# A select over a pad behind each gather, in place of the waits for landings

## The chip, the cores and the metric
The kernel runs on one core of one Trainium2 chip. The metric is the device time of one execution in microseconds. TensorE (PE) multiplies, VectorE (DVE) and ScalarE (ACT) evict and reduce, GpSimd (POOL) builds the indirect transfers, SyncE (SP) starts the plain ones.

## The reference
2048 samples, 40 categorical fields with 64 numbers each. For every pair of fields (780) and every sample a bilinear form is computed, then a small dense tower:

```python
e = jnp.stack([tbl_f[ids[:, f]] for f in range(40)], axis=1)     # (2048, 40, 64), written out in the reference
out = jnp.einsum('bie,fie,bif->bi', e[:, rowidx], param, e[:, colidx])   # 780 pairs, param (64, 780, 64)
h = jnp.concatenate([out, dense_ctx], axis=1)                    # (2048, 796)
h = jnp.maximum(h @ W_top1 + b_top1, 0.0)                        # 512
h = jnp.maximum(h @ W_top2 + b_top2, 0.0)                        # 256
y = h @ W_top3
```

Everything is float32.

## The kernel before
The batch is cut into four chunks of 512 samples (`NB`), each into four tiles of 128 (`BT`). Two fields make one tile `m` of 20. For chunk `c`, tile `m` the rows of two tables are fetched by 8 indirect DMAs (gathers), 4 for each of the two fields `f`, each of 128 rows of 64 numbers, into `rows[:, slot, t, ...]` (line 481). Tiles 4 to 7 of chunk 0 (`ONE_HOT`) are not gathered: their small tables are loaded whole, VectorE builds one-hot matrices (`one_hot`, line 647), and TensorE multiplies them with the tables (line 690). That leaves 76 gathered tiles, 608 gathers, in the order of `GATHERED`.

TensorE transposes a gathered tile (`transpose_tile`, line 701) when all its 128 counts have come (`pe.wait_ge(gathered[slot], use * 2 * BT * 16)`, line 698), and ScalarE copies it to `e_t` (line 502). A list `ITEMS`, written out ahead, fixes the order of the work on TensorE, VectorE and ScalarE; `TILE_AT` says before which item a tile is transposed. In chunk 0 the order of tiles is 4, 5, 6, 7, 0, 1, 2, 3 and then 8 to 19.

The items are "units" (line 727, two matmuls each, then VectorE multiplies into `prod`, lines 603 and 606, and TensorE sums with `strip` in `z_ps`, line 750) and "wides" for the pairs with tiles 0 to 3 (line 732, VectorE multiplies into `wide_prod`, line 619, ScalarE sums with an accumulator, line 541, in chunk 0 sometimes VectorE, line 630). No wide can start before tile 3 of its chunk is transposed. After each chunk the tower runs (lines 756, 760, 763, evicted at 550 and 553).

Weights come in pieces of up to 768 KB into three slots (`W_SLOTS`), started by SyncE when TensorE has used up the piece three before (line 421). Index lists are double-buffered by chunk (line 424).

GpSimd's whole program is the function below. At the start it makes `ident` and `first_row`. Then for each gathered tile it waits until the slot is free: tiles 0 to 3 have slots of their own for even and odd chunks, the others go round in six (`G_SLOTS`), each free when TensorE has transposed the tile that was in it (line 477). Then come four gathers of the first field and a wait until they have landed, four of the second and a wait until those have landed (line 487; only the very first four go without). Each gather adds 16 to the slot's semaphore when it has landed.

Of the kernel before, what the change touches and what calls it, by code (L numbers as in the profile page):

```python
# [7 lines left out]
ALU = mybir.AluOpType  # L8
# [3 lines left out]
P = 128  # L12
# [8 lines left out]
BT = NB // P  # L21
# [151 lines left out]
def through(n):  # L173

    return 2 * (n + 1)
# [78 lines left out]
def slot_of(tile):  # L254


    c, m = divmod(tile, TILES)
    if m < FIXED:
        return fixed_slot(c) + m, c // 2 + 1
    n = c * (TILES - FIXED) + m - FIXED - len(ONE_HOT)  # L260
    return 2 * FIXED + n % G_SLOTS, n // G_SLOTS + 1
# [78 lines left out]
def bilinear_tower(nc, tables, idx, hot_ids, dense_t, weights, w1z, b1c, w2p, b2c, w3c, out):  # L340
    with ExitStack() as ctx:
        def sb(name, shape, dt=F32):
            return ctx.enter_context(nc.sbuf_tensor(name, shape, dt))
# [4 lines left out]
        def sem(name):  # L348
            return ctx.enter_context(nc.semaphore(name))
# [15 lines left out]
        h2 = sb("h2", [P, KH2, NB])  # L365
        ident = sb("ident", [P, P])
        strip = sb("strip", [P, 62])
        first_row = sb("first_row", [P, 1], I32)
        first_row_f = sb("first_row_f", [P, 1])

# [15 lines left out]
        gathered = [sem(f"gathered{i}") for i in range(2 * FIXED + G_SLOTS)]  # L386
        w_in = [sem(f"w_in{i}") for i in range(W_SLOTS)]
        dense_in = sem("dense_in")
        hot_in = [sem(f"hot_in{i}") for i in range(len(ONE_HOT))]
        hot_ready = sem("hot_ready")  # L390
        hot_used = sem("hot_used")
        rows_known = sem("rows_known")
# [23 lines left out]
        @block.sync  # L416
        def _(sp):
            def load(piece):
                slot = piece % W_SLOTS
                start, n, _ = PIECES[piece]  # L420
                sp.dma_start(w[:, slot, :n * P], weights[:, start * P:(start + n) * P]).then_inc(w_in[slot], 16)

            def load_idx(c):
                sp.dma_start(idx_now[:, c % 2, :], idx[:, c * IDX:c * IDX + IDX]).then_inc(idx_in, 16)

            def load_tables(i):

                for h in range(2):
                    table = tables[2 * ONE_HOT[i] + h].rearrange("(p j) e -> p (j e)", j=HOT_J)
                    for part in (slice(0, HOT_SPLIT), slice(HOT_SPLIT, HOT_P)):  # L430
                        sp.dma_start(z_t[part, 2 * i + h, :], table[part, :]).then_inc(hot_in[i], 16)

            load_idx(0)
            for i in range(2):
                load_tables(i)
            load(0)
            for i in range(2, len(ONE_HOT)):
                load_tables(i)

            sp.wait_ge(transposed, T_NUMBER[0] + 1)  # L440
            load_idx(1)
            for piece in range(1, W_SLOTS):
                load(piece)
            for piece in range(W_SLOTS, len(PIECES)):

                sp.wait_ge(t_ready, through(PIECES[piece - W_SLOTS][2]))
                load(piece)
                if piece == MLP_BEHIND:
                    for dst, src in ((b1[:, :], b1c), (b2[:, :], b2c), (w3[:, :], w3c), (w2[:, :, :], w2p),
                                     (w1[:, :], w1z)):  # L450
                        sp.dma_start(dst, src).then_inc(mlp_in, 16)
                for c in range(2, CHUNKS):
                    if piece == IDX_BEHIND[c]:

                        sp.wait_ge(transposed, (c - 1) * TILES)
                        load_idx(c)

        @block.gpsimd
        def _(pool):
            nc.gpsimd.memset(ident[:, :], 0.0).then_inc(consts, 1)  # L460
            pool.wait_ge(consts, 1)
            nc.gpsimd.affine_select(out=ident[:, :], in_=ident[:, :], compare_op=ALU.not_equal, fill=1.0,
                                    base=0, pattern=[[-1, P]], channel_multiplier=1).then_inc(consts, 1)
            nc.gpsimd.iota(first_row[:, :], [[1, 1]], base=0, channel_multiplier=HOT_J).then_inc(rows_known, 1)
            pool.wait_ge(idx_in, 16)
            for tile in GATHERED:
                c, m = divmod(tile, TILES)
                slot, use = slot_of(tile)
                if c > 0 and m == 0:
                    pool.wait_ge(idx_in, 16 * (c + 1))  # L470
                if m < FIXED and use > 1:

                    pool.wait_ge(t_free, through(PLACE[c - 2, "wide", NW - 1]))
                elif use > 1:

                    last = max(t for t in GATHERED if t < tile and slot_of(t)[0] == slot)
                    pool.wait_ge(transposed, T_NUMBER[last] + 1)
                for f in range(2):
                    for t in range(BT):
                        col = (m * 2 + f) * BT + t  # L480
                        nc.gpsimd.indirect_dma_start(  # L481
                            out=rows[:, slot, t, E * f:E * f + E], out_offset=None, in_=tables[m * 2 + f],
                            in_offset=bass.IndirectOffsetOnAxis(ap=idx_now[:, c % 2, col:col + 1], axis=0),
                        ).then_inc(gathered[slot], 16)
                    if c > 0 or m > 0 or f > 0:

                        pool.wait_ge(gathered[slot], 16 * BT * (f + 1 + 2 * (use - 1)))

        @block.scalar
        def _(act):  # L490
# [69 lines left out]
            for n in range(ALL_ITEMS + max(GROUP_LAG) + 1):  # L560
                for tile in TILES_AT.get(n, ()):
                    prepare(tile)
                if n == NI:
                    act.wait_ge(mlp_in, 5 * 16)
                if n in STEPS_AT:
                    finish_step(*STEPS_AT[n])
                if n in TURNS_AT and n < ALL_ITEMS:
                    copy_half(TURNS_AT[n])
                for c, t in Z_ORDER:
                    if t < ZS and group_at(c * GROUPS + Z_FIRST[t + 1] - 1) == n:  # L570
                        copy_z(c, t)
                done = n - REDUCE_LAG
                if 0 <= done < ALL_ITEMS and ITEMS[done][1] == "wide":
                    c, _, v = ITEMS[done]
                    if not reduced_by_vector(c, v):
                        reduce(c, v)
# [334 lines left out]
```

## Time and profile before

| what | value |
|---|---|
| median of 3 runs | 1275.0 us (1274.24 to 1276.26) |
| profiled execution | 1274.63 us, span 1272.8 us |
| TensorE busy | 1231.0 us, 97% |
| VectorE, ScalarE busy | 1023.4 and 1023.9 us, 80% each |
| GpSimd busy | 577.7 us, 45%, of which 608 gathers 576.9 us |
| mean granted TensorE clock | 0.993 |

The span is the time from the first to the last instruction of the profiled execution. GpSimd's busy time counts the making of the transfers' descriptors, not the transfers. "Idle before" in a group of instructions is the time the engine stood still ahead of them, with the releaser that ended it; "issue" is a gap for which the profile shows no wait. The chain of waits follows what released what back from the last instruction. Only what stands on it sets the time.

### The profile page before, as it was taken

To read this page: it belongs to the slowest core of one execution; us is meant where nothing else is said; L and a number is where in the kernel's file an instruction comes from. 1 tells how busy PE (TensorE), PEld (TensorE's weight loads), DVE (VectorE), ACT (ScalarE), POOL (GpSimd) and SP (SyncE) were. 2 spreads that over 40 slices of the span, in tenths; PEclk is the share of its full clock that TensorE was granted. 3 is DMA by queue.
4 is the path that set the end of the run, shared out by engine and by line. 5 is a ranking of instruction groups with operands and counts; after the bars stand their busy time and mean duration, and the time that the engine had idled before them with its cause. 6 is when DMAs were issued, how large, how long until landed. Compare 5 with 4: busy or idle time off the path is not lost.

```text
span 1272.8 us, 23705 instructions
## 1 busy us (share of the span) xinstructions
PE 1231.0 (97%) x6064; PEld 481.1 (38%) x6064; DVE 1023.4 (80%) x1680; ACT 1023.9 (80%) x7945; POOL 577.7 (45%) x615
## 2 busy tenths in 40 slices
PE   6788999999999999999999999999999999999999
PEld 3233433333333343333344333433343333343333
DVE  5768999998887777888787887788889787788980
ACT  0049988777488989998958999899968898999981
POOL 5555555555555555555345555555225554000000
PEclk9989999999999999999999999999999999999999
DMA  6311422132221222222221222122112122111100
GB/s 173 94 46 46 143 72 70 45 94 64 71 70 48 70 71 70 49 67 64 66 67 47 73 69 71 45 70 72 54 59 69 46 70 67 30 47 50 44 2 0
DMA packets 33201, 80.88 MB, mean 64 GB/s; under 512 B 11773, under 2 KB 12285, under 8 KB 32937
## 3 DMA queue, kind: packets, MB, share of 16 engines
q1 hardware_dynamic: 12320, 57.17, 13.9%
q0 software_dynamic: 19456, 19.96, 7.7%
q10 hardware_dynamic: 1288, 2.24, 0.6%
q8 instruction: 48, 0.79, 0.3%
q14 instruction: 89, 0.72, 0.2%
HBM read 79.32 MB, written 0.01 MB: 62 GB/s over the span
## 4 chain that ended last, share of the span: by engine, by line
PE 60%; ACT 31%; issue 3%; DMA 2%; POOL 2%; DVE 1%; another core or an unknown queue 1%; ACTq 0%
ACT wide_prod L541 29%; PE ring L727 26%; PE z_ps L750 13%; PE ring L732 11%; PE ring L756 7%; DMA rows<-tbl,idx_now 2%; POOL rows L481 2%; PE ring L701 2%; ACT e_t L502 1%; PE ring L760 1%; DMA idx_now<-idx 0%; DVE prod L606 0%; PE ring L763 0%; PE ring L708 0%
## 5 line engine op out<-in xcount | busy, mean ns | idle before, releaser
L541 ACT ACTIVATE wide_prod<-wide_prod 128x64 f32<-128x64 f32 x3904 | 933.7, 243 | 52.4 <-DVE wide_prod L619 25.6
L481 POOL DMA_INDIRECT rows<-tbl,idx_now x608 | 576.9, 949 | 496.7 <-DMA rows<-tbl,idx_now 292.2
L541 ACT ACTIVATION_READ_ACCUMULATOR wide_prod<-wide_prod 128x1 f32 x3904 | 739.4, 189 | 24.4 <-issue 23.4
L606 DVE TENSOR_TENSOR prod<-ring,e_t 128x512 f32<-128x512 f32 x1008 | 630.8, 683 | 147.6 <-PE ring L727 101.1
L727 PE MATMUL ring<-e_t,w 64*128 64x512 f32 x2176 | 563.0, 609 | 9.6 <-ACT e_t L502 5.9
L619 DVE TENSOR_TENSOR wide_prod<-ring,rows 128x512 f32<-128x512 f32 x512 | 328.3, 682 | 44.6 <-PE ring L732 33.3
L727 PEld LDWEIGHTS ring<-e_t,w 64*128 64x128 f32 x2176 | 215.9, 187 | 300.1 <-issue 203.7
L732 PE MATMUL ring<-w,e_t 64*128 64x512 f32 x1024 | 292.1, 607 | 11.4 <-ACT e_t L502 7.1
L750 PE MATMUL z_ps<-prod,strip 128*32 128x512 f32 x2096 | 256.2, 603 | 0.1
L732 PEld LDWEIGHTS ring<-w,e_t 64*128 64x128 f32 x1024 | 106.2, 186 | 147.0 <-issue 86.7
L750 PEld LDWEIGHTS z_ps<-prod,strip 128*32 128x32 f32 x2096 | 55.3, 109 | 182.0 <-issue 119.6
L502 ACT ACTIVATE e_t<-ring 128x512 f32<-128x512 f32 x80 | 44.7, 587 | 90.7 <-PE ring L701 47.9
L756 PE MATMUL ring<-z_t,w 128*128 128x512 f32 x224 | 99.8, 598 | 0.0
L756 PEld LDWEIGHTS ring<-z_t,w 128*128 128x128 f32 x224 | 41.4, 190 | 56.8 <-issue 49.2
L603 DVE TENSOR_TENSOR prod<-ring,e_t 64x512 f32<-64x512 f32 x80 | 54.8, 685 | 6.2 <-PE ring L727 3.9
L701 PE MATMUL ring<-ident,rows 128*128 128x128 f32 x304 | 45.5, 284 | 7.8 <-DMA rows<-tbl,idx_now 7.8
L701 PEld LDWEIGHTS ring<-ident,rows 128*128 128x128 f32 x304 | 32.5, 142 | 49.8 <-issue 41.2
L514 ACT ACTIVATE z_t<-z_ps 128x512 f32<-128x512 f32 x20 | 11.8, 588 | 38.8 <-PE z_ps L750 30.1
L690 PE MATMUL ring<-wide_prod,z_t 125*64 125x512 f32 x128 | 30.5, 631 | 10.7 <-DMA z_t<-tbl 10.7
L550 ACT ACTIVATE h<-ring,b 128x512 f32<-128x512 f32 x16 | 10.9, 683 | 27.9 <-PE ring L756 27.8
L647 DVE TENSOR_SCALAR wide_prod<-h,first_row_f 125x512 f32<-125x512 int32 x48 | 20.4, 490 | 12.1 <-DMA z_t<-tbl 8.3
L760 PE MATMUL ring<-h,w 128*128 128x512 f32 x64 | 29.2, 602 | 0.0
(23 smaller groups left out, 79.3 us busy)
## 6 DMA issues: line engine op xcount, KB each, us to landing
w<-weights SPq DMA_DIRECT2D x64, 768.0 KB
rows<-tbl,idx_now POOLq DMA_INDIRECT x608
w<-weights SPq DMA_DIRECT2D x4, 512.0 KB
z_t<-tbl SPq DMA_DIRECT2D x8, 224.0 KB
w<-w1z SPq DMA_DIRECT2D x1, 1792.0 KB
h<-hot_ids ACTq DMA_DIRECT2D x6, 256.0 KB
z_t<-hot_ids ACTq DMA_DIRECT2D x2, 256.0 KB
w<-w2p SPq DMA_DIRECT2D x1, 512.0 KB
```

The source lines that it names most:

```text
L481: nc.gpsimd.indirect_dma_start(out=rows[:, slot, t, E * f:E * f + E], out_offset=None, in_=tables[m * 2 + f], in_offset=bass.IndirectOffse ...
L502: nc.scalar.activation(e_t[:, m, :], ring[:, BANKS["tile", tile][0], :], ACT.Copy).then_inc(e_ready, 1)
L541: last = nc.scalar.activation(products, products, ACT.Copy, accum_out=z_b[:, h, t, col:col + 1])
L603: nc.vector.tensor_tensor(dst[half, 0, :], ring[half, bank, :], e_t[half, m - 1 + j, :], ALU.mult).then_inc(t_free, 1)
L606: nc.vector.tensor_tensor(dst[:, j, :], ring[:, bank, :], e_t[:, k, :], ALU.mult).then_inc(t_free, 1)
L619: nc.vector.tensor_tensor(dst[:, j, :, :], src[:, bank, :, :], rows[:, fixed_slot(c):fixed_slot(c) + FIXED, t, :], ALU.mult).then_inc(t_fr ...
L701: last = nc.tensor.transpose(dst[:, P * t:P * t + P], rows[:, slot, t, :], ident[:, :])
L727: nc.tensor.matmul(dst, w[field, slot, P * o:P * o + P], e_t[field, m - 1 if diagonal and b == 0 else m, :], start=True, stop=True).then_i ...
L732: nc.tensor.matmul(dst, e_t[field, m, P * t:P * t + P], w[field, slot, P * o:P * o + FIXED * P], start=True, stop=True).then_inc(t_ready, 1)
L750: last = nc.tensor.matmul(z_ps[32 * col:32 * col + 32, :], strip[:, 30 - 2 * r:62 - 2 * r], prod[:, (c * NU + UNIT_PLACE[c][u]) % PROD_SLO ...
L756: return nc.tensor.matmul(dst, w1[:, t * H1 + P * h:t * H1 + P * h + P], z_t[:, Z_NUMBER[c, t] % Z_SLOTS, :], start=start, stop=stop)
L760: return nc.tensor.matmul(dst, w2[:, k, P * h:P * h + P], h1[:, k, :], start=k == 0, stop=k == KH1 - 1)
```

## The change
The two landing waits per tile go. In their place GpSimd runs one select over a 128x256 float32 tensor `pad` behind each gather, that is 608 of them. Nobody reads `pad`. Each select waits for the one before it (semaphore `paced`), since it writes what it reads. The other waits of GpSimd (index lists, free slots) are as before, and so is TensorE's wait for a whole tile.

```diff
+        pad = sb("pad", [P, 2 * P])
...
+        paced = sem("paced")
...
+            nc.gpsimd.memset(pad[:, :], 0.0).then_inc(paced, 1)
+            paused = 1
             pool.wait_ge(idx_in, 16)
...
                         ).then_inc(gathered[slot], 16)
-                    if c > 0 or m > 0 or f > 0:
-
-                        pool.wait_ge(gathered[slot], 16 * BT * (f + 1 + 2 * (use - 1)))
+
+                        pool.wait_ge(paced, paused)
+                        nc.gpsimd.affine_select(out=pad[:, :], in_=pad[:, :], compare_op=ALU.not_equal, fill=1.0, base=0,
+                                                pattern=[[-1, 2 * P]], channel_multiplier=1).then_inc(paced, 1)
+                        paused += 1
```

## Rows read from the trace of the kernel before

**Rows 1.** The page: busy us, share of the span, instructions of each engine.
```profile
PE 1231.0 (97%) x6064; PEld 481.1 (38%) x6064; DVE 1023.4 (80%) x1680; ACT 1023.9 (80%) x7945; POOL 577.7 (45%) x615
```

**Rows 2.** The page: the chain that ended last, by engine.
```profile
PE 60%; ACT 31%; issue 3%; DMA 2%; POOL 2%; DVE 1%; another core or an unknown queue 1%; ACTq 0%
```

**Rows 3.** The chain in order of time: start us, us, what.
```profile
63.18 2.44 DMA rows<-tbl,idx_now
```

**Rows 4.** GpSimd's waits (us in total, times, longest) and line 481's durations.
```profile
POOL rows L481 <- DMA rows<-tbl,idx_now: 292.2, 142, 5.9
POOL rows L481 <- issue: 139.3, 457, 0.3
POOL rows L481 <- PE ring L701: 55.6, 5, 28.8
...
L481 POOL DMA_INDIRECT rows<-tbl,idx_now x608: 938/944/1316, 4.9 to 1074.2; - x152
```

**Rows 5.** Timeline of TensorE, 44 to 80 us: start us, us, instruction, idle before.
```profile
55.88 1.99 PE L727 MATMUL ring<-e_t,w 64*128 64x512 f32 x8 [0.69 <-ACT e_t L502]
65.67 1.12 PE L701 MATMUL ring<-ident,rows 128*128 128x128 f32 x4 [7.80 <-DMA rows<-tbl,idx_now]
67.47 2.08 PE L727 MATMUL ring<-e_t,w 64*128 64x512 f32 x4 [0.69 <-ACT e_t L502]
69.47 3.64 PE L750 MATMUL z_ps<-prod,strip 128*32 128x512 f32 x16
...
75.87 1.92 PE L750 MATMUL z_ps<-prod,strip 128*32 128x512 f32 x16
```

**Rows 6.** Timeline of GpSimd: gathers 1, 32, 33 and 208.
```profile
4.92 1.11 POOL L481 DMA_INDIRECT rows<-tbl,idx_now  x1 [3.37 <-DMA idx_now<-idx]
...
63.18 0.94 POOL L481 DMA_INDIRECT rows<-tbl,idx_now  x1 [0.30 <-issue]
65.88 0.94 POOL L481 DMA_INDIRECT rows<-tbl,idx_now  x1 [1.75 <-DMA rows<-tbl,idx_now]
...
356.81 0.94 POOL L481 DMA_INDIRECT rows<-tbl,idx_now  x1 [0.30 <-issue]
```

**Rows 7.** Timeline of GpSimd, its first instructions.
```profile
0.25 0.10 POOL L898 MEMSET const-float32-0.0<- 128x1 f32 x1 [0.25 <-issue]
...
0.74 0.20 POOL L460 MEMSET ident<- 128x128 f32 x1 [0.29 <-POOLq L898]
1.19 0.28 POOL L462 TENSOR_SCALAR_AFFINE_SELECT ident<-ident 128x128 f32<-128x128 f32 x1 [0.24 <-POOL ident L460]
1.44 0.12 POOL L464 IOTA first_row<- 128x1 int32 x1
```

**Rows 8.** Line 647, the one-hots: ns least/median/most, first and last start.
```profile
L647 DVE TENSOR_SCALAR wide_prod<-h,first_row_f x48: 468/481/689, 10.1 to 33.8; 125x512 f32<-125x512 int32 x48
L647 DVE TENSOR_SCALAR wide_prod<-z_t,first_row_f x16: 478/480/689, 36.9 to 43.4; 125x512 f32<-125x512 int32 x16
```

**Rows 9.** Groups by line, GpSimd, 4 to 43.8 us.
```profile
L481 POOL DMA_INDIRECT rows<-tbl,idx_now x21 | 23.2, 1103 | 19.1 <-DMA rows<-tbl,idx_now 10.9 <-issue 4.9 <-DMA idx_now<-idx 3.4
```

**Rows 10.** Stretches: us, busy PE, PEld, DVE, ACT, POOL (x), granted clock, DMA share, GB/s.
```profile
58.00:63.00 5.00, 0.00 (x0) 0.00 (x0) 1.52 (x3) 0.00 (x0) 2.83 (x3) 0.99 0.55 173
63.00:73.30 10.30, 6.95 (x26) 2.07 (x28) 0.12 (x1) 0.60 (x1) 5.60 (x6) 0.51 0.11 21
```

**Rows 11.** Timeline of TensorE: transposes of chunk 1, tiles 8 and 9, then 11.
```profile
363.25 1.09 PE L701 MATMUL ring<-ident,rows 128*128 128x128 f32 x8
...
392.83 0.66 PE L701 MATMUL ring<-ident,rows 128*128 128x128 f32 x4
```

**Rows 12.** Groups by line, VectorE: 200 to 300 us, then 1080 to 1170 us; engines in 200:300.
```profile
L606 DVE TENSOR_TENSOR prod<-ring,e_t 128x512 f32<-128x512 f32 x112 | 69.5, 682 | 3.5 <-PE ring L727 3.4
...
L606 DVE TENSOR_TENSOR prod<-ring,e_t 128x512 f32<-128x512 f32 x75 | 47.2, 683 | 13.4 <-PE ring L727 13.4
...
200.00:300.00 100.00, 100.00 (x554) 38.51 (x551) 94.62 (x156) 79.62 (x628) 55.87 (x60) 1.00 0.24 67
```

## The prediction

> **What bounds the kernel now.** I read the page first. TensorE is busy 97% of the span, VectorE and ScalarE 80% each, GpSimd 45% [rows 1]. The chain that ended last gives TensorE and ScalarE 91% of the span and the gathers, DMA and GpSimd together, only 4% [rows 2]. Its pieces in order of time say where that 4% lies: the last landing on it begins at 63.18 with tile 3's last gather and ends at 65.62; after that there are only matmuls, evictions and reductions [rows 3]. So the gathers decide when the dense part starts, and nothing later, as long as none of them comes late.
>
> GpSimd's waits look large, 292.2 us for landings in 142 waits, 139.3 us of "issue" in 457 gaps, 55.6 us for slots that TensorE has not emptied [rows 4]. Almost none of it is on the path: TensorE waits for a landing once, 7.80 us, before it transposes tile 3 at 65.67 [rows 5]. What the change can win is inside that one wait and the slow clock around it. What it can lose is the lead of the gathers over TensorE further on.
>
> **What GpSimd does per gather now.** In a quiet stretch the timeline shows 0.94 us for a gather, 0.30 us until the next, and after four of them a landing wait of about 1.7 us [rows 6]. That is 3 x 1.24 + 0.94 + 1.75 = 6.41 us for four, 1.60 each. Some waits are longer, up to 5.9 us [rows 4], so that from 65.88 (33rd gather) to 356.81 (208th) the mean is 290.93/175 = 1.66, and from 4.92 to 63.18 (32 gathers) it is 58.26/31 = 1.88 [rows 6].
>
> **Removed.** 151 landing waits, the 142 that cost something together 292.2 us of GpSimd's time [rows 4]. Nothing on another engine read them; TensorE has its own wait on the same counts.
>
> **Added.** 608 selects of 128x256, each behind a wait for the select before it. That wait is for an instruction that ended a whole gather earlier, so I cost it at nothing; were its cover gone it would be the 0.24 us that stand between the ident memset and its select [rows 7]. The select itself is not in the trace at this size. At 128x128 it takes 0.28 us, the 128x1 memsets 0.10 to 0.12, so 128 columns cost about 0.17, and 256 columns 0.28 + 0.17 = 0.45 [rows 7]. The iota behind it starts 0.03 before the select's end, so what it occupies is about 0.42. Bounds: below, 0.28 + (0.20 - 0.10), the memset's slope, less 0.03 = 0.35; above, twice the 128x128 one, 0.56. I take 0.42.
>
> The gaps are the disputed term. The 0.30 us between two gathers may lie behind a gather (then it stays once), before a gather (then it can hide under the select), or on both sides of any pair (then it comes twice). After a landing, and likewise after the memset, an instruction starts 0.24 to 0.26 us after what it waited for, whatever it is; the iota starts behind the select with no gap. I take the gap once. Pace: 0.94 + 0.30 + 0.42 = 1.66, bounds 0.94 + 0.35 = 1.29 and 0.94 + 0.60 + 0.56 = 2.10. A useful way to see the change: the pace of before is 1.60 and stalls on top, the new one 1.66 and none.
>
> The Trainium skill ("GPSIMD Engine Reference", Performance pitfalls for Q7 kernels) has a compare-and-select loop at 1.03 to 2.03 cycles an element at 1.2 GHz: 0.22 to 0.43 us for 256 columns. By its lower figure the pace would be an estimated 1.46, by its upper 1.67; the row's slope, 0.17 for 128 columns, is 1.3 ns a column and stands nearer the upper one.
>
> **The start.** VectorE builds the one-hot tables from 10.09 to 44.12 with 64 instructions of about 0.48 us, up to 0.69; gathers beside them go from 0.944 up to 1.316 [rows 8, 4]. Over the first 21 gathers their mean is 1.103, so that is 21 x 0.159 = 3.3 us in all [rows 9]. It stays. The selects may be held up too: some 17 fall beside these instructions; at none it costs 0, at a whole 0.48 each it costs 8. I take 0.13 each, 2.2, for 5.5 together (bounds 3.3 and 11.5). Tile 3 lands with its 32nd gather, 2.44 us after its start [rows 3]:
>
> 4.92 + 31 x 1.66 + 5.5 + 2.44 = 64.3 us, 1.3 us before today's 65.62.
>
> Tiles 0 to 2 are no limit: TensorE's one landing wait was for tile 3, and tile 2 would be there eight gathers, 13 us, before it, at about 51, while TensorE is still at work up to 57.87 [rows 5].
>
> Then the clock. TensorE does nothing from 58 to 63 us, the granted clock falls, and from 63.0 to 73.3 it is 0.51, the 1.2 GHz level [rows 10]. The work in it is slow: four L727 matmuls 2.08 us against half of 1.99, sixteen L750 3.64 against 1.92, the transpose 1.12 against 0.66, together 3.3 us on the chain [rows 5]. Tile 3 comes 1.3 us earlier and the work before it somewhat later (VectorE's one-hots are held up by the selects as well), so the idle stretch is shorter. No row shows whether the clock then holds; bounds are 0 and 3.3 and I take 2.5. Gain at the start: 1.3 + 2.5 = 3.8 us. Behind it ScalarE's reductions and TensorE's matmuls make up the chain, 91% of it, so it is carried to the end [rows 2].
>
> **The lead further on.** The tightest place is chunk 1, tile 9, the 26th gathered: last gather at 356.81, transposed as the second of the two that begin at 363.25, so at about 363.7 [rows 6, 11]. Its landing would be 4.92 + 207 x 1.66 + 5.5 + 2.44 = 356.5; TensorE wants it at 363.7 - 3.8 = 359.9. It holds by 3.4 us. Tile 11 (223 intervals) lands at 383.0, wanted at 389.0 [rows 11]. Later on GpSimd is ahead and waits for slots, 55.6 us in five waits [rows 4]; these waits grow or shrink and cost nothing.
>
> **VectorE beside the selects.** Its product instructions take 0.682 us where GpSimd gathers (200 to 300 us) and 0.683 where it has ended (1080 to 1170) [rows 12], so gathers cost them nothing. Selects, which also read SBUF, are not in these rows. VectorE is over 94% busy from 200 to 300 us [rows 12]. The Trainium skill ("SBUF — State Buffer", SBUF: two separate sides) says that GpSimd and VectorE exclude each other for a whole instruction on a shared pair of ports when VectorE is in a 2-port mode or has two SBUF inputs. The products here have one operand in PSUM; by that rule they are free, and the one-hots are not if theirs is a 2-port mode, which no row says.
>
> **Sum.** 1274.63 for the profiled execution (span 1272.8 and 1.8 around it), less 3.8 is 1270.8. The median of the runs, 1275.0, is 0.4 above the profiled one: 1271.2.
>
> **Rivals.**
> *The pace is too slow (slower).* The lead at chunk 1 tile 9 is 363.7 - 356.81 - 2.44 = 4.4 us today. With pace p its landing moves by 207 p: it is late against today from p = (363.7 - 12.9)/207 = 1.695, only 0.035 above my value. At 1.75 it lands at 375.1, 11.4 late, at 1.80 21.8 late, and TensorE, which bounds that stretch, passes it to the end: 1286 and 1297. For it: a wait in front of the select, a second gap. Against: the iota's missing gap. 26%.
> *GpSimd is much quicker.* The gap hides under the select, p about 1.4 to 1.5; then tile 3 is there before TensorE is through with the earlier work, and the whole 7.8 us of the wait and the 3.3 us of clock go: 1264. 13%.
> *No change.* The one-hot stretch eats the start: with 7.5 us instead of 5.5 and p = 1.68 tile 3 lands at 66.9, the clock falls as before: 1275 to 1276. The same if a full queue makes GpSimd wait inside the gather, so that landings still set the pace and the change does not do what it says: gathers of 1.3 us, also 1275. 22%.
> *The selects hold up VectorE's products.* 60 gathers in 200:300, 0.42 each, are 25 us on an engine with under 6 us to spare; over the stretches that dense, some 300 us, at least 60 us: 1335. 5%.
>
> **How the numbers follow.** Forecast 34%, rivals 26, 13, 22 and 5. What a measurement of this kernel tells from no change is about 0.2%, 2.5 us. Faster: the forecast's and the quick case, 47%. Same: 22%. Slower: 31%. The range reaches down to the quick case, 1264, and up to a pace of about 1.77, 1291; the forecast's own range is 1267 to 1273. Beyond both ends there are 2 in 10.
>
> **What would show it.** The distance of two gathers in a quiet stretch: 1.66. Select duration: 0.45. TensorE's one landing wait: about 5 us instead of 7.80, ending near 64. The granted clock in 63 to 73: if 1.0, the 2.5 is right. No landing wait of TensorE near 360; if there is one, the pace was above 1.695, and the time is slower by 207 times the excess. L606 still at 0.682; if not, the last rival. The prediction is wrong above all if the pace misses by more than 0.035 upwards.

## The result and the profile after

| | changed kernel | kernel before |
|---|---|---|
| median of 5 runs | 1328.94 us (1327.18 to 1346.17) | 1274.24 us (1267.79 to 1276.26) |
| ratio, 95% interval | 1.0456 [1.0411, 1.0501] | |
| profiled execution, span, mean clock | 1346.17, 1344.3, 0.981 | 1274.63, 1272.8, 0.993 |

A ratio and its interval leave out runs over 1.5% above the fastest of the same kernel; a median is that of all runs.

The change costs 4.6%, outside the predicted range and on the other side. The page of the changed kernel has these answers to [rows 1, 2] (busy us by engine, then the chain that ended last):

```profile
PE 1277.6 (95%) x6064; PEld 494.3 (37%) x6064; DVE 1032.9 (77%) x1680; ACT 1023.9 (76%) x7945; POOL 826.7 (61%) x1224
...
PE 71%; ACT 20%; another core or an unknown queue 3%; DVE 2%; issue 2%; DMA 1%; SPq 0%; ACTq 0%; DVEq 0%
```

The same 6064 matmuls take 46.6 us more. No second core takes part, so "another core or an unknown queue", now 3% of 1344 us, means updates of a semaphore whose source the profile does not find. The timeline of GpSimd in a quiet stretch, where [rows 6] had the gathers (start us, us, instruction, idle before it):

```profile
64.68 0.94 POOL L485 DMA_INDIRECT rows<-tbl,idx_now  x1 [0.16 <-POOL pad L491]
65.63 0.41 POOL L491 TENSOR_SCALAR_AFFINE_SELECT pad<-pad 128x256 f32<-128x256 f32 x1
66.20 0.94 POOL L485 DMA_INDIRECT rows<-tbl,idx_now  x1 [0.16 <-POOL pad L491]
67.16 0.41 POOL L491 TENSOR_SCALAR_AFFINE_SELECT pad<-pad 128x256 f32<-128x256 f32 x1
```

A gather starts every 1.53 us (median 1.526), without a pause. TensorE's timeline around tile 3, for [rows 5], and the stretches of [rows 10, 12] (us; busy PE, PEld, DVE, ACT, POOL; granted clock; DMA share; GB/s):

```profile
56.69 0.65 PE L707 MATMUL ring<-ident,rows 128*128 128x128 f32 x4
58.03 1.99 PE L733 MATMUL ring<-e_t,w 64*128 64x512 f32 x8 [0.69 <-ACT e_t L508]
60.16 0.66 PE L707 MATMUL ring<-ident,rows 128*128 128x128 f32 x4
61.51 1.13 PE L733 MATMUL ring<-e_t,w 64*128 64x512 f32 x4 [0.69 <-ACT e_t L508]
62.56 1.92 PE L756 MATMUL z_ps<-prod,strip 128*32 128x512 f32 x16
```
```profile
58.00:63.00 5.00, 4.14 (x20) 1.57 (x24) 3.02 (x5) 0.60 (x1) 4.47 (x7) 1.00 0.80 266
63.00:73.30 10.30, 10.30 (x68) 3.50 (x64) 8.05 (x14) 1.77 (x15) 9.09 (x14) 1.00 0.19 52
200.00:300.00 100.00, 92.06 (x436) 33.84 (x428) 74.66 (x122) 63.98 (x506) 88.23 (x131) 0.93 0.23 62
```

The start did what it should, and more: no landing wait, the clock at 1.00. But from 200 to 300 us TensorE does 436 matmuls where it did 554, with gaps and at a lower clock, and VectorE is busy 74.66 us where it was 94.62 [rows 12].

Set matmul against matmul, the nth of this trace minus the nth of before, the time is not lost evenly: -8.7 us at 80 us of before's time, -10.0 at 120, then +0.8 at 180, +13.0 at 220, +28.1 at 280. It hardly moves from 300 to 360 (+28 to +27), stands at +52 from 500 to 560, falls to +43 from 560 to 650, and stays at +71.5 from 1080 to the end. In more than half of each of the first three GpSimd waits for slots, and in the last it has finished. The kernel loses time only in stretches in which it gathers without pause, though not in all of those.

One such loss, VectorE's timeline and then TensorE's at 219 to 228 us:

```profile
220.61 1.28 DVE L612 TENSOR_TENSOR prod<-ring,e_t 128x512 f32<-128x512 f32 x2
225.61 1.29 DVE L612 TENSOR_TENSOR prod<-ring,e_t 128x512 f32<-128x512 f32 x2 [3.73 <-PE ring L733]
```
```profile
221.62 1.02 PE L738 MATMUL ring<-w,e_t 64*128 64x512 f32 x4
222.48 1.88 PE L733 MATMUL ring<-e_t,w 64*128 64x512 f32 x6
226.36 3.27 PE L733 MATMUL ring<-e_t,w 64*128 64x512 f32 x6 [2.00 <-DVE prod L612]
```

VectorE stands still for 3.73 us, TensorE after it 2.00, and then six matmuls take 3.27 us where 12 take 2.85 at full clock (the granted clock is 0.67 from 226.3 to 229.6). The profile says VectorE waited for TensorE's matmuls. The trace's semaphore records say for what: the two matmuls that it needs ended at 221.78 and 221.79, but TensorE's updates `t_ready` are recorded at 225.52 and 225.56, between landings of a gather (225.51, 225.55, 225.57). The z sums ended at 220.73 and their update `summed` came at 224.77. ScalarE's `reduced_s` stands at 225.53 for work that ended at 224.98. The work was done; the news of it was late, by 3.7 to 4.0 us from TensorE and 0.55 us from ScalarE, and it came out in bunches.

I use one measure for this below, from those records: how long after the last matmul of a group of z sums ends its update `summed` is recorded, and how many groups are late by over 1 us. Groups are counted that end within 2.5 us of a gather's start; a few whose update has no record before the next group ends are left out. Before: mean 0.56 us, 27 of 102 late. After: mean 1.78 us, 47 of 83 late. For the groups away from gathers it is 0.04 to 0.05 us in both. So the kernel before had the fault too, about half as often and a third as much on average; its landing waits held it down.

A second count needs no semaphore record: how often VectorE stands idle for over 1 us although the matmul that its next product reads has ended (the nth product against the nth matmul that updates `t_ready`). Before: 9 times, 14.7 us in all. After: 38 times, 101.0 us.

Not every engine's news is late. In the same trace, while gathers run, 606 of GpSimd's 608 updates have a record of their own, within 0.011 us of the instruction's end. Of VectorE's some 1200 about 770 have one, within 0.012 us; of the others the trace can't tell. Late are TensorE's (up to 5.3 us) and, much less, ScalarE's (up to 1.1).

GpSimd's waits for slots grew against [rows 4], since TensorE empties them later, and so did VectorE's waits for TensorE. First the changed kernel, then VectorE's line of before (total us, times, longest):

```profile
POOL rows L485 <- PE ring L707: 189.7, 13, 36.9
DVE prod L612 <- PE ring L733: 137.5, 82, 5.0
...
POOL rows L485 <- POOL pad L491: 96.9, 586, 0.7
```
```profile
DVE prod L606 <- PE ring L727: 101.1, 93, 5.0
```

### The profile page after: what moved, and what is told of

It reads as the page before. It is cut to its first block, busy times and chain, and to the rows that moved or that the text cites. A ratio compares the mean times of both kernels' runs of the same rounds, so it can differ in the third digit from the quotient of the medians.

```text
span 1344.3 us, 24860 instructions
## 1 busy us (share of the span) xinstructions
PE 1277.6 (95%) x6064; PEld 494.3 (37%) x6064; DVE 1032.9 (77%) x1680; ACT 1023.9 (76%) x7945; POOL 826.7 (61%) x1224
## 4 chain that ended last, share of the span: by engine, by line
PE 71%; ACT 20%; another core or an unknown queue 3%; DVE 2%; issue 2%; DMA 1%; SPq 0%; ACTq 0%; DVEq 0%
PE ring L733 31%; ACT wide_prod L547 19%; PE z_ps L756 14%; PE ring L738 13%; PE ring L762 7%; PE ring L707 2%; PE ring L696 2%; PE ring L766 2%; DVE prod L612 1%; ACT e_t L508 1%; DVE wide_prod L625 1%; DMA z_t<-tbl 1%; DVE prod L609 0%; PE ring L714 0%
## 5 line engine op out<-in xcount | busy, mean ns | idle before, releaser
L733 PE MATMUL ring<-e_t,w 64*128 64x512 f32 x2176 | 591.9, 615 | 35.2 <-DVE prod L612 18.5
L733 PEld LDWEIGHTS ring<-e_t,w 64*128 64x128 f32 x2176 | 224.0, 188 | 339.1 <-issue 205.0
L738 PE MATMUL ring<-w,e_t 64*128 64x512 f32 x1024 | 307.4, 616 | 17.5 <-issue 8.6
L756 PE MATMUL z_ps<-prod,strip 128*32 128x512 f32 x2096 | 261.6, 614 | 0.0
L491 POOL TENSOR_SCALAR_AFFINE_SELECT pad<-pad 128x256 f32<-128x256 f32 x608 | 251.3, 413 | 5.2
L738 PEld LDWEIGHTS ring<-w,e_t 64*128 64x128 f32 x1024 | 110.1, 188 | 158.9 <-issue 98.1
L653 DVE TENSOR_SCALAR wide_prod<-h,first_row_f 125x512 f32<-125x512 int32 x48 | 25.6, 610 | 8.9 <-DMA z_t<-tbl 8.4
```

Source lines behind the costliest of these rows:

```text
L491: nc.gpsimd.affine_select(out=pad[:, :], in_=pad[:, :], compare_op=ALU.not_equal, fill=1.0, base=0, pattern=[[-1, 2 * P]], channel_multipl ...
L733: nc.tensor.matmul(dst, w[field, slot, P * o:P * o + P], e_t[field, m - 1 if diagonal and b == 0 else m, :], start=True, stop=True).then_i ...
L738: nc.tensor.matmul(dst, e_t[field, m, P * t:P * t + P], w[field, slot, P * o:P * o + FIXED * P], start=True, stop=True).then_inc(t_ready, 1)
L756: last = nc.tensor.matmul(z_ps[32 * col:32 * col + 32, :], strip[:, 30 - 2 * r:62 - 2 * r], prod[:, (c * NU + UNIT_PLACE[c][u]) % PROD_SLO ...
```

## The experiments

The expectations name the theories they tell apart. Each kernel is compared with the kernel before on the same chip in the same sitting; the sittings are called occasions A to E below, and it turned out to matter which one a number is from.

### Occasion A: is it the missing pause or the selects?

Chip 7; the kernel before took 1274.08 us. `k1_bare` is the kernel before without landing waits:

```diff
-                    if c > 0 or m > 0 or f > 0:
-                        pool.wait_ge(gathered[slot], 16 * BT * (f + 1 + 2 * (use - 1)))
```

> Neither landing waits nor selects: GpSimd issues gathers back to back, 1.24 us apart, until the slots are full. Theory A (a stream of gathers without a pause delays the semaphore updates of TensorE and ScalarE, and a pause in which all have landed ends the delay): slower than before, 1300 to 1345, the updates late in the trace as in the changed kernel. Theory B (the selects do it, by their SBUF traffic or their semaphore): the start is won (8 to 11 us) and nothing is lost, 1262 to 1268.

**1789.74 us, ratio 1.4057 [1.3994, 1.4119].** Four of its costliest waits (total us, times, longest):

```profile
POOL rows L481 <- PE ring L698: 784.7, 39, 55.2
...
DVE prod L603 <- remote: 229.9, 35, 16.7
...
POOL rows L481 <- issue: 172.5, 566, 0.3
DVE wide_prod L616 <- remote: 157.6, 19, 25.9
```

With no select anywhere, gathers 1.25 us apart, VectorE's products wait 387 us for "remote" (an update whose source the profile does not find), up to 25.9 us at a time; 35 of 56 updates are late. The missing pause alone does the damage, and much more of it than with selects in between.

`k2_wait_one` keeps the landing waits and puts one select behind every fourth gather (the memset of `pad` and `paced` as in the change):

```diff
                         ).then_inc(gathered[slot], 16)
+                    pool.wait_ge(paced, paused)
+                    nc.gpsimd.affine_select(out=pad[:, :], in_=pad[:, :], ..., pattern=[[-1, 2 * P]], channel_multiplier=1).then_inc(paced, 1)
+                    paused += 1
```

> Landing waits kept as before, one select behind every fourth gather, inside the landing wait that is there anyway (152 selects). Theory A: as before, 1272 to 1277. Theory B: a quarter of the changed kernel's loss of some 60 to 80 us, so about 1290.

**1277.26 us, 1.0023 [0.9995, 1.0052].** 152 selects beside the waits cost nothing that shows.

`k3_block` has no landing waits; three selects stand in a row behind every fourth gather, where the wait stood:

```diff
+                    for _ in range(3):
+                        pool.wait_ge(paced, paused)
+                        nc.gpsimd.affine_select(out=pad[:, :], in_=pad[:, :], ..., pattern=[[-1, 2 * P]], channel_multiplier=1).then_inc(paced, 1)
+                        paused += 1
```

> No landing waits; three selects in a row behind every fourth gather instead of one behind each (456 selects), so that the fourth gather has landed when the next begins, at a mean pace near 1.6 us. Theory A: the pause is there, about as before, 1268 to 1280. Theory B: three quarters of the loss, 1310 to 1330.

**1274.17 us, 0.9995 [0.9968, 1.0022].** A pause of 1.5 us of selects works as the landing wait does, at 0.75 of the change's selects. As in before, part of the updates stay late (37 of 98).

`k4_wait8` is the changed kernel with one landing wait per tile put back:

```diff
                         paused += 1
+                    if f == 1:
+                        pool.wait_ge(gathered[slot], 16 * BT * (f + 1 + 2 * (use - 1)))
```

> The changed kernel with its select behind each gather and, in addition, one landing wait per tile (every 8 gathers). Theory A: a pause every 13 us instead of every 6.4, between the two kernels, 1285 to 1310. Theory B: as the changed kernel or a little slower, 1325 to 1340.

**1264.38 us, 0.9919 [0.9891, 0.9946]**, 6 of 100 late. With all 608 selects in it, one wait in eight gathers turns 1.0456 (measured on another occasion) into a gain. So the selects are innocent; the missing pause does it. TensorE now waits for landings 19.6 us, 14.3 of them between 330 and 400 us, around chunk 1 tile 9, as the slower rival had it, but here through the wait.

### Occasion B: how dense may it be?

Chip 4; before 1247.81 us. `k5_wait8_pad128` is `k4_wait8` with a smaller pad, so gathers are 1.42 us apart between the waits:

```diff
-        pad = sb("pad", [P, 2 * P])
+        pad = sb("pad", [P, 128])
```

> A select behind each gather, but of 128x128 (gathers about 1.39 us apart instead of 1.53), and one landing wait per tile. Gathers come earlier than in the run with 128x256 and the same wait, which had TensorE waiting 19.6 us for landings. If the spacing of gathers within a run of eight matters little, 1245 to 1260, faster than that run. If closer gathers hold the other engines' semaphore updates longer, the gain is eaten: 1264 to 1290.

**1231.8 us, 0.9877 [0.9842, 0.9912]**, none of 108 late.

`k6_pad384` is the changed kernel with 384 columns for 256 in the pad and in the select's pattern; select 0.51 us, gathers 1.63 apart, no wait:

```diff
-        pad = sb("pad", [P, 2 * P])
+        pad = sb("pad", [P, 384])
```

> The changed kernel with a select of 128x384 instead of 128x256: no landing waits, gathers about 1.66 us apart. Theory A1 (only a moment at which all gathers have landed ends a delay; with a landing 2.4 us after its start there is none at this distance either): about as the changed kernel, 1315 to 1340. Theory A2 (the distance itself counts, each gather takes 1.2 to 1.5 us of something that the updates of the others need): 1265 to 1295.

**1229.15 us, 0.9862 [0.9827, 0.9896]**, none late.

`k7_two128` has two selects of 128x128 behind each gather:

```diff
+                        for _ in range(2):
+                            pool.wait_ge(paced, paused)
+                            nc.gpsimd.affine_select(..., pattern=[[-1, 128]], channel_multiplier=1).then_inc(paced, 1)
+                            paused += 1
```

> The changed kernel with two selects of 128x128 behind each gather: no landing waits, gathers about 1.76 us apart, still never all landed. Theory A1: delays as in the changed kernel and late gathers on top, above 1330. Theory A2: the delays are small and short; what is left is the lateness of the gathers worked out in the prediction, 207 x (1.76 - 1.695) = 13 us at chunk 1, less the start: 1275 to 1290.

**1438.09 us, 1.1534 [1.1494, 1.1574]**, meant to be as dense as the change. It is not. GpSimd's timeline, then a wait of TensorE:

```profile
201.26 0.94 POOL L485 DMA_INDIRECT rows<-tbl,idx_now  x1 [0.38 <-POOL pad L492]
202.22 0.74 POOL L492 TENSOR_SCALAR_AFFINE_SELECT pad<-pad 128x128 f32<-128x128 f32 x2
203.34 0.95 POOL L485 DMA_INDIRECT rows<-tbl,idx_now  x1 [0.38 <-POOL pad L492]
```
```profile
PE ring L708 <- DMA rows<-tbl,idx_now: 174.9, 19, 16.0
```

The second select waits for the one just ahead, and the gap behind is 0.38 instead of 0.16: 2.07 us a gather. None of 117 updates is late; this is the prediction's slower rival in pure form, gathers that come too late. Its formula, 207 x (2.07 - 1.695) = 78 us by chunk 1 tile 9, stands against +86.7 measured at 380 us of the traced kernel before. It does not end there: +163.4 at the end, since later gathers come late as well.

`k8_bare_wait8` is the kernel before with one landing wait per tile instead of two, no selects, 1.25 us between gathers:

```diff
-                    if c > 0 or m > 0 or f > 0:
+                    if f == 1:
```

> The kernel before with one landing wait per tile (every eight gathers) instead of two, no selects; gathers 1.25 us apart within a run of eight. Theories A1 and A2 both: a delay can last a whole run, 9 to 10 us instead of 4 to 5, so slower than before by much, 1320 to 1450. Theory B (the selects): the start is won, 1262 to 1270.

**1224.78 us, 0.9825 [0.9791, 0.9859]**, none late. That broke the theory as it stood: here dense gathers did no harm. But the kernel before also was 26 us faster than on occasion A.

### Occasion C: the same programs again

Chip 12; before 1274.12 us. `k9_before` is the kernel before, traced again; `k10_after` the changed kernel; `k11_pad384` is `k6_pad384`; `k12_bare_wait8` is `k8_bare_wait8`, word for word:

```diff
k9_before, k10_after, k11_pad384, k12_bare_wait8: no edit against before, the change, k6_pad384, k8_bare_wait8
```

> The kernel before, unchanged, for its trace beside those of the next three on one chip. Chips so far differ: 1274 on one, 1248 on the other. If late semaphore updates are what the slower chip adds, its trace has them (mean lateness of the sums' update 0.6 us or more while gathers run) where it takes 1274 and nearly none where it takes 1248 or less.

> The changed kernel, unchanged, again. Theory C (the lateness depends on the chip as much as on the stream of gathers): on a chip where the kernel before takes 1274 it takes about 1329 again; on one where that takes 1248 it has no late updates and takes 1225 to 1235, faster than before. Theory A without the chip: 4 to 5% slower than before on either.

> The changed kernel with a select of 128x384, which was 1.4% faster than before on a chip where before takes 1248. If the chip is of the other kind (1274): theory A1 (no moment without an outstanding gather, so delays as in the changed kernel) 1310 to 1340; theory A2 (the distance of the gathers decides) 1240 to 1275. If it is of the same kind: 1229 again.

> The kernel before with one landing wait per tile and no selects, which was 1.8% faster on a chip where before takes 1248. If the chip is of the other kind: theories A1 and A2 have it slower than before, 1320 to 1450; if the landing wait alone is enough, 1250 to 1274. If it is of the same kind: 1225 again.

| kernel | us | ratio | late |
|---|---|---|---|
| k9_before | 1274.42 | 0.9997 [0.9980, 1.0015] | 33 of 104 |
| k10_after | 1338.17 | 1.0500 [1.0466, 1.0534] | 47 of 81 |
| k11_pad384 | 1229.26 | 0.9652 [0.9631, 0.9673] | 0 of 92 |
| k12_bare_wait8 | 1691.93 (1668.87 to 1701.72) | 1.33, from the medians | 46 of 64 |

The same program took 1224.78 us on occasion B and 1691.93 here, while the one with 1.63 us between gathers took 1229.15 and 1229.26. It is not the mean pace that counts: `k3_block`, with three gathers in four 1.25 us apart and a pause of 1.78 us behind the fourth, has a mean of 1.62 us and 37 of 98 updates late (A), `k11_pad384`, evenly 1.63 us apart, none (C). So two things decide: the distance of the gathers, and something that differs between occasions and that a wide distance makes harmless.

### Occasion D: where is the threshold?

Chip 4 again; before 1261.18 us. Pads of 192, 320 and 416 columns, and a memset in the select's place:

```diff
-        pad = sb("pad", [P, 2 * P])
+        pad = sb("pad", [P, 192])      # k13; 320 in k14, 416 in k15 and k16; the select's pattern alike
...
-                        nc.gpsimd.affine_select(out=pad[:, :], in_=pad[:, :], ...).then_inc(paced, 1)
+                        nc.gpsimd.memset(pad[:, :], 0.0).then_inc(paced, 1)      # k16 alone
```

> The changed kernel with a select of 128x192: gathers about 1.46 us apart. Theory A2 (the shorter the distance, the longer the updates are held): worse than 128x256, 1360 to 1500 on a chip where before takes 1274. If it is a matter of the size 256 alone (a coincidence of two rhythms): 1225 to 1300.

> The changed kernel with a select of 128x320: gathers about 1.58 us apart, between 1.53 (1329 to 1338) and 1.63 (1229). Theory A2: between them, 1229 to 1290, nearer the fast end if there is a threshold.

> The changed kernel with a select of 128x416: gathers about 1.665 us apart. Theory A2: no late updates; the lateness of gathers begins, since TensorE now wants chunk 1, tile 9 at 363.7 - 13.9 = 349.8 and 4.92 + 207 x 1.665 + 2.44 = 352.0: 1230 to 1238.

> The changed kernel with a memset of 128x416 in place of the select of 128x256: about 0.43 us, so nearly the same distance (1.53 to 1.56), but it reads nothing. If the distance decides: about as the changed kernel, 1290 to 1340 on a chip where before takes 1274. If the select's reading does it: 1229 to 1245.

| kernel | filler, us | distance, us | us | ratio | late |
|---|---|---|---|---|---|
| k13_pad192 | 0.356 | 1.476 | 1408.84 | 1.1042 [1.0986, 1.1098] | 51 of 80 |
| k16_memset416 | 0.459 | 1.575 | 1229.49 | 0.9746 [0.9726, 0.9765] | 0 of 87 |
| k14_pad320 | 0.462 | 1.579 | **1228.06** | 0.9735 [0.9716, 0.9754] | 0 of 87 |
| k15_pad416 | 0.540 | 1.659 | 1234.86 | 0.9791 [0.9771, 0.9811] | 0 of 74 |

At 0.05 us beyond the change's 1.526 the loss is gone and a gain of 2.7% stands in its place; the loss at 1.526 itself is from other occasions, and within this one it lies at 1.476. What fills 1.58 us, a select or a memset that reads nothing, does not matter. At a distance that does harm the two were not compared; there the selects are cleared by `k1_bare`, which has none, and by `k11_pad384`, whose selects are longer. The engines' busy times of `k14_pad320`:

```profile
PE 1204.4 (98%) x6064; PEld 468.6 (38%) x6064; DVE 1028.4 (84%) x1680; ACT 1011.0 (82%) x7945; POOL 860.0 (70%) x1224
```

TensorE is busy 98% of a span of 1226.3, so the gathers have little left to give. At 1.659 TensorE's waits for landings are back, 3.6 us in two.

### Occasion E: the change itself, once more

Chip 11; before 1248.44 us. `k17_after` is the changed kernel; `k18_memset352` puts a memset of 352 columns in the select's place and so keeps the distance (1.521 us):

```diff
-        pad = sb("pad", [P, 2 * P])
+        pad = sb("pad", [P, 352])      # k18 alone
...
+                        nc.gpsimd.memset(pad[:, :], 0.0).then_inc(paced, 1)      # k18 alone, for the select
```

> The changed kernel as it stands (select over 128x256, gathers 1.53 us apart), the partner of the next run on the same chip. Theory A2 (the distance from gather to gather decides, whatever fills it): slower than before, about 1.04 to 1.06 times, with the updates of TensorE late behind more than 60 of some 100 z sums. Rival B (the select itself, which reads and writes the pad, delays the updates): the same for this run.

> The changed kernel with a memset over 128x352 in place of the select over 128x256, sized so that the gathers stay some 1.52 to 1.54 us apart; the memset only writes. A2: as slow as the changed kernel beside it, ratio 1.03 to 1.07, over 50 late updates. B: with no select and no read of the pad the updates come in time, ratio 0.965 to 0.985 as with the wider memset (0.9746). If the distance comes out over 1.56 us, the run says nothing and both expect 0.965 to 0.985.

**`k17_after` 1226.52 us, 0.9843 [0.9800, 0.9886]; `k18_memset352` 1228.18, 0.9856 [0.9813, 0.9899].** None of 103 updates is late in either. Both theories missed: on this occasion the changed kernel is 1.6% faster than before, with gathers just as dense. Its stretch from 200 to 300 us, then its waits of VectorE and GpSimd (total us, times, longest):

```profile
200.00:300.00 100.00, 100.00 (x566) 37.69 (x562) 93.99 (x155) 74.71 (x594) 88.18 (x131) 1.00 0.27 75
```
```profile
DVE prod L612 <- PE ring L733: 108.0, 94, 5.3
POOL rows L485 <- POOL pad L491: 98.0, 592, 0.7
...
POOL rows L485 <- PE ring L707: 84.5, 9, 26.4
```

GpSimd does what it did in the result's trace (88.18 us and 131 instructions against 88.23 and 131 in this stretch), and TensorE does 566 matmuls instead of 436. The line of the page on the gathers' transfers differs between the occasions, `k10_after` first, then `k17_after` (the last number is the median from issue to landing):

```profile
rows<-tbl,idx_now POOLq DMA_INDIRECT x608
```
```profile
rows<-tbl,idx_now POOLq DMA_INDIRECT x608, 2.5
```

The profile can't pair issues with landings in the first, because fewer updates are recorded: 5,234 by the DMA engines in `k10_after`, 11,255 in `k17_after`, for the same transfers. It is so for whole occasions: 11,198 to 11,313 in all kernels of B and E; 3,573 to 7,316 in those of C and D, 2,883 to 6,531 in A, 5,507 and 5,403 in the traces of the result. The two traces of the 384-column pad, equal in time, have 11,198 (B) and 6,979 (C). So it marks the occasion, not the loss. I read a missing record as an increment that arrived together with another; that is a reading, not shown.

## Why the prediction was wrong

**The failed step is "Removed": since nothing on another engine read the landing waits, taking them away was given no effect outside GpSimd.** That nothing reads them is true; that they have no effect is not. They were pauses in a stream of gathers, and on four of the occasions (the result's, A, C and D) TensorE's semaphore updates, and to a lesser degree ScalarE's, came the later the closer the gathers stood. With the pauses, 27 of 102 updates came over 1 us late; without, 47 of 83 at 1.53 us from gather to gather. Late updates start VectorE late, so TensorE idles, its clock is granted at 0.93 in 200:300, and 71.5 us are lost in the profiled pair. `k1_bare` (remove the waits alone, 1.41), `k4_wait8` (one of two waits put back beside the selects: 0.992) and `k11_pad384` (a wider distance: 0.965) show it from three sides. VectorE's idle starts behind matmuls that had ended go the same way: 9 and 14 in the two traces of before, 38 and 39 in the bad ones of the change, 65 in `k1_bare`, 109 in `k12_bare_wait8`, one in every kernel at 1.575 us or more and in every kernel of B and E.

Point by point:
- **Pace 1.66.** Measured 1.526. The gather 0.94 and the select (0.407 median, 0.42 taken) were right. The disputed gap was taken once, at 0.30; it is 0.16 behind the select and 0.01 ahead of it, 0.17 in all. The wait on `paced` costs nothing here, as said; where it has no cover (`k7_two128`) it costs 0.17 inside the pair and 0.22 more behind it.
- **The lead, and the slower rival.** It held: no matmul waits for a landing of a gather any more; one weight load does, 1.0 us. The rival's sign came true by another mechanism, which is no merit of it. Its own price was about right in `k7_two128` for chunk 1 (78 us against 86.7) and half of the whole loss (163.4). The prediction made a *slower* GpSimd the danger and a quicker one a gain of about 11 us, when the quicker pace was the harm.
- **The start, -3.8.** Measured -8.7 at 80 us. The whole 7.80 wait and the half clock went, as in the quick rival, because the 32nd gather started at 54.00 and not at the 61.9 of the working: the pace is 0.13 us shorter over 31 gathers, and what comes on top is 2.1 us, below the bounds of 3.3 to 11.5. The clock's term lay at its upper bound, 3.3. Against these 11.1 us stands TensorE's work ahead of tile 3, which came 2.2 later (58.03 for 55.88, below). VectorE's one-hots took 0.608 us instead of 0.481:

```profile
L653 DVE TENSOR_SCALAR wide_prod<-h,first_row_f x48: 472/608/765, 10.1 to 35.5; 125x512 f32<-125x512 int32 x48
L491 POOL TENSOR_SCALAR_AFFINE_SELECT pad<-pad x608: 406/407/542, 5.7 to 1126.5; 128x256 f32<-128x256 f32 x152
```
```profile
L485 POOL DMA_INDIRECT rows<-tbl,idx_now x25 | 23.8, 952 | 6.7 <-POOL pad L491 3.9 <-DMA idx_now<-idx 2.8
L491 POOL TENSOR_SCALAR_AFFINE_SELECT pad<-pad 128x256 f32<-128x256 f32 x24 | 11.6, 482 | 0.2
```

  The first two lines are the one-hots and the selects over the whole run (ns least/median/most, first and last start), the others GpSimd's groups in 4:44. There the 24 selects take 0.482, 1.8 us in all for 2.2 forecast; the gathers take 0.952 and not 1.103, so the 3.3 us of [rows 9] went too. The sum charged the selects to GpSimd alone: 64 one-hots at 0.127 more are 8 us on VectorE. TensorE's last L727 group ahead of tile 3 starts at 58.03 and not at 55.88 [rows 5]; that these 2.2 us come from them is likely, no run shows it.
- **VectorE's products.** Unchanged, 0.683 us: that rival is out. The Trainium skill ("SBUF — State Buffer", SBUF: two separate sides) lets GpSimd and VectorE exclude each other only when VectorE is in a 2-port mode or reads two SBUF inputs. By that rule the products, with one operand in PSUM, are free, and the trace agrees (0.683). The one-hots are slowed, 0.608 for 0.481; the rule would need a 2-port mode for that, which no row names.
- **The sum.** It had no term for what one engine's stream does to the others' updates, because the trace of before was read by engine and by wait only. The signs were in it: nine times VectorE stood idle 1.0 to 3.7 us behind matmuls that had ended (its longest waits, 5.0 us, are no sign; their matmuls had just ended, and `k17_after` has them too), "another core or an unknown queue 1%" in [rows 2] on a program of one core, and TensorE busy 1231.0 us for work that takes 1203.2 in `k17_after`.

**How far the verdict reaches.** 1.0456 and 1.0500 were measured on two occasions, 0.9843 on a third. Where before takes 1274, the change loses; where it takes 1248, it gains. Had I forecast for occasion E, 1226.5 would still be a gain of 22 us instead of 3.8. How these 22 divide between the start and before's own late updates is open, since before was not traced there.

**What stays open.** What in the chip holds TensorE's updates, while those of VectorE and GpSimd that are recorded come in time, and what differs between occasions. Not the chip alone: before took 1247.81 and 1261.18 us on chip 4, and `k5` to `k8` had their full records there and `k13` to `k16` not. The packets don't differ: their median time is 56 ns in `k11_pad384` and in `k6_pad384`, 60 in `k10_after` and 66 in `k17_after`. Whether the records that the profiler writes have a part in it, no run tests. The threshold, between 1.526 (C) and 1.575 us (D), is put together from two occasions; within one it is known only to lie between 1.476 and 1.575 (D), or between 1.526 and 1.633 (C).

**The better version** is the change with 320 columns: 1228.06 us, 0.9735 [0.9716, 0.9754] where it was measured, on D alone. The pad of 384 columns took 1229.15 on B and 1229.26 on C, which makes it the one that was tried on a good and on a bad occasion. `k17_after` and `k8_bare_wait8` are 2 to 4 us faster on good occasions, and the same programs took 102 to 467 us more on bad ones.

## What to carry to other kernels

A wait that looks idle can be what spaces out an engine's transfers: before it goes, ask how dense the stream gets without it, and look in the trace of before whether other engines' waits end at the work they name or some microseconds later. Where the pause has to go, a filler of fixed length sets the distance, and the distance wants a margin (here 1.58 to 1.63 us from gather to gather) rather than a fit. Measure a change of this kind on more than one chip and hour; a sign that turns from +5.0% to -1.6% is not visible in five runs at one sitting.

## What the runs showed of the hardware

- The update behind a group of TensorE's z sums is recorded 0.04 to 0.05 us after the last matmul without gathers, and 1.78 us after it on average beside gathers 1.53 us apart (result's trace); on occasion E beside the same gathers it is 0.04. GpSimd's updates are recorded within 0.011 us in the result's trace, and VectorE's within 0.012 where they have a record. The Trainium skill ("DMA: Bandwidth & Descriptors", Why a DMA increments its semaphore by 16 and not by 1) says that every gather from GpSimd brings 16 increments, one from each DMA engine. That makes 608 x 16 = 9728 here, an estimate by that page. The traces agree as far as they go: `k17_after` holds 9,621 of them, the result's 4,420. No run varies their number.
- Damage against density on bad occasions: gathers 1.25 us apart 1.41 (A) and, with a wait in eight, 1.33 (C); 1.48 apart 1.104 (D); 1.53 apart 1.046 and 1.050; 1.575 and 1.579 apart 0.975 and 0.974 (D); 1.63 apart 0.965 (C).
- GpSimd's select over 128 rows: 0.407 us for 256 columns, 0.462 for 320, 0.51 for 384, 0.540 for 416, that is 0.83 ns a column beyond 256; a memset of 416 columns takes 0.459.
- GpSimd's gap between two gathers is 0.30 us, but 0.16 behind a select, and 0.38 behind a select that had to wait for one just ahead.
